# Edge sort of a graph network: bias by ScalarE, groups of four, and columns written a step later

## The reference

```
gate = sigmoid(silu(rbf @ W1 + b1) @ W2 + b2)     # rbf: edge_attr_64, 50000 x 64
msg  = gate * h[src]
aggr = segment_sum(msg, dst)
```

## Time and profile before

| what | value |
|---|---|
| three timed runs | 4744.28, 4751.31, 4754.04 us; median 4751.31 |
| profiled execution | span 4744.9 us from first to last instruction; the page gives no other time of it |
| busy over the span | TensorE 3915.0 us (83%), VectorE 3382.7 (71%), GpSimd 3071.7 (65%), ScalarE 1791.0 (38%) |
| the second pass of the sort | first matmul of its first group at 174.66 us, last scatter issued at 777.05 us |

### The profile page before, as it was taken

How to read it: one execution, slowest core, us unless ns; L and a number is a source line. 1 busy time by engine, 2 the same in 40 slices (tenths; PEclk the granted TensorE clock), 3 DMA queues, 4 the chain that set the end, 5 groups by cost and what they waited for, 6 DMA issues and landing times. The chain is left out here.

```text
span 4744.9 us, 105920 instructions
## 1 busy us (share of the span) xinstructions
PE 3915.0 (83%) x22300; PEld 3233.3 (68%) x22301; DVE 3382.7 (71%) x9318; ACT 1791.0 (38%) x5399; POOL 3071.7 (65%) x3178
## 2 busy tenths in 40 slices
PE   6799997889987889878899566779978778578886
PEld 3477775778776778767777556668866666366664
DVE  7799997667757778677787667874257778756666
ACT  0355553221123333333333100004257667367774
POOL 0266665777756777567775777766777773067774
PEclk9799998999998999989999777888978898778787
DMA  1233334856626445264452687861465444144445
GB/s 47 92 131 131 130 132 130 212 126 158 152 63 202 135 145 154 71 185 146 145 149 78 208 257 214 245 191 54 145 182 120 105 106 125 32 99 109 109 109 100
DMA packets 643665, 643.00 MB, mean 136 GB/s; under 512 B 314342, under 2 KB 549540, under 8 KB 643396
## 3 DMA queue, kind: packets, MB, share of 16 engines
q0 software_dynamic: 145840, 374.54, 27.8%
q1 hardware_dynamic: 443348, 213.36, 17.0%
q10 hardware_dynamic: 54336, 53.65, 3.3%
HBM read 470.09 MB, written 170.26 MB: 135 GB/s over the span
## 5 line engine op out<-in xcount | busy, mean ns | idle before, releaser
L1059 POOL DMA_INDIRECT G<-h_dram,idx x1572 | 1525.8, 971 | 556.8 <-issue 361.6
L1283 PEld LDWEIGHTS ps_a<-hotm,msg 128*128 128x128 f32 x4716 | 686.5, 193 | 196.2 <-DVE arena L1395 67.5
L1283 PE MATMUL ps_a<-hotm,msg 128*128 128x128 f32 x4716 | 730.0, 282 | 88.5 <-DVE arena L1395 87.8
L1271 PE MATMUL ps_e<-nnw,attT 128*128 128x256 f32 x2358 | 738.4, 396 | 76.8 <-DVE prodm L1388 42.4
L1395 DVE TENSOR_TENSOR arena<-ps_a,arena 128x256 f32 x1404 | 586.9, 418 | 218.8 <-issue 94.1
L735 POOL DMA_INDIRECT rec_dram<-rec,pos x392 | 376.7, 961 | 398.6 <-ACT rec L606 307.7
L1059 POOL DMA_INDIRECT G<-feat_dram,idx x420 | 402.4, 958 | 325.5 <-POOLq L241 197.9
L1317 ACT ACTIVATE msg<-prodm 128x256 f32<-128x256 f32 x786 | 327.5, 417 | 677.8 <-DVE prodm L1388 586.1
L749 POOL DMA_INDIRECT rec_dram<-rows,place x392 | 379.8, 969 | 222.1 <-issue 117.4
L1897 POOL DMA_INDIRECT arena<-rel_dram,idx x393 | 385.0, 980 | 128.6 <-issue 86.2
L1271 PEld LDWEIGHTS ps_e<-nnw,attT 128*128 128x128 f32 x2358 | 370.3, 195 | 118.4 <-DVE prodm L1388 56.4
(11 more groups left out here) (365 smaller groups left out, 7691.6 us busy)
## 6 DMA issues: line engine op xcount, KB each, us to landing
gate<-rec_dram SPq DMA_DIRECT2D x126, 384.0 KB
G<-msg_dram SPq DMA_DIRECT2D x300, 128.0 KB, 2.2
msg_dram<-msg ACTq DMA_DIRECT2D x270, 128.0 KB
rel_dram<-stage SPq DMA_DIRECT2D x25, 1040.0 KB
G<-h_dram,idx POOLq DMA_INDIRECT x1572
aT<-edge_attr SPq DMA_DIRECT2D x98, 128.0 KB
msg_dram<-arena ACTq DMA_DIRECT2D x90, 128.0 KB
attT<-attT_dram SPq DMA_DIRECT2D x74, 144.0 KB
```

Of the source, the lines that this page charges most:

```text
L1059: pool.indirect_dma_start(G[:, n % width, :], None, table, bass.IndirectOffsetOnAxis(ap=idx[:, which, n:n + 1], axis=0)).then_inc(sem(f"sw ...
L1271: t.matmul(ps_e[s % BANKS][:], attT[:, s // HU, s % HU, :], nnw[:], start=True, stop=True).then_inc(sem("ew"), 1)
L1283: last = t.matmul(ps_a[s % BANKS][:, h, :], of[:, h * P:(h + 1) * P], hot[:, s, :], start=True, stop=True)
```

## The change

In the second pass of the sort:

- The unit of the gate is the whole group. Lags are 0 and 1, `walk` has width 2. `sig` and `silu` hold four columns and move into the arena.
- ScalarE copies b2, now loaded to all partitions, into each `ps_g` bank after the gate has been taken from it; L641 and the three bf16 parts of b2 go. One matmul per bank of zeros comes once, at the start.
- One-hots of both keys are one comparison against `keys4` (the destination key three times, the source key once) and are made one step ahead.
- Fields, places and the copy of the 32 attributes are written in the step after their group's first layer. The places by source are kept as sums in `pos_s` and turned to integers once at the end.
- SyncE's wait and the loads are the same, with units of groups.

```diff
+                keys4 = area(4 * (EC + SG)).rearrange("p (c f) -> p c f", f=4)
+                pos_s = area(EC)
-                        for q in range(3):
-                            sp.dma_start(b2[32 * q:32 * q + 1, :], ...)
+                        sp.dma_start(b2[:], L1_gnn_b2.rearrange("(a d) -> a d", a=1).to_broadcast([P, D])).then_inc(sem("w_in"), 16)
...
+                def first_layer(b, h):
+                    return ps_z[b][:].rearrange("p j (q h e) -> p j q h e", q=2, h=DH)[:, :, :, h, :]
+                def by_pairs(of, b, h):
+                    return of[:, b, h, :, :].rearrange("p (j q) e -> p j q e", j=2)
... SyncE
-                                wait_ahead(sp, (sem("z"), upto(g * 2 + 1 - PAIRS)), (sem("a32"), upto(g - 2)))
+                                wait_ahead(sp, (sem("z"), upto(g - 2)), (sem("a32"), upto(g - 2)))
... ScalarE
+                        for c0, c1 in walk(nc.scalar, NG // 2, 0, 1, width=2):
+                            if c0:
+                                act.wait_ge(sem("z"), upto(g))
+                                act.wait_ge(sem("silu"), upto(g - 2))
+                                for h in range(DH):
+                                    last = nc.scalar.activation(by_pairs(sig, b, h), first_layer(b, h), ACT.Sigmoid, bias=b1[:, h:h + 1])
+                            if c1:
+                                for q in range(2):
+                                    if q == 0:
+                                        ... wait for sw_rec of the four columns
+                                        act.wait_ge(sem(f"attr_in{b}"), i * 32 + 32)
+                                    act.wait_ge(sem("g"), g * 2 + q + 1 + CREDIT)
+                                    nc.scalar.activation(rec[:, b, 2 * q:2 * q + 2, 0:D], ps_g[q][:], ACT.Sigmoid).then_inc(sem("gate"), 1)
+                                    act.wait_ge(sem("gate"), g * 2 + q + 1 + CREDIT)
+                                    nc.scalar.copy(ps_g[q][:], bias2).then_inc(sem("seeded"), 1)
+                                    if q == 0:
+                                        nc.scalar.copy(rec[:, b, :, WA32:WA32 + A32], at32[:, b, :, :]).then_inc(sem("a32"), 1)
... TensorE
+                        for c0, c1 in walk(nc.tensor, NG // 2, 0, 1, width=2):
+                            if c0:
+                                pe.wait_ge(sem("hot"), g + 1)
+                                ... the three rank matmuls
+                                pe.wait_ge(sem(f"attr_in{b}"), i * 32 + 32)
+                                pe.wait_ge(sem("silu"), upto(g - 2))
+                                ... first layer of four columns
+                            if c1:
+                                pe.wait_ge(sem("silu"), upto(g))
+                                for q in range(2):
+                                    pe.wait_ge(sem("seeded"), g * 2 + q + 1)
+                                    ... second layer of two columns
+                            if c0:
+                                pe.wait_ge(sem("looked_up"), g + 1)
+                                ... the four counting matmuls
... VectorE
+                        for c0, c1 in walk(nc.vector, NG // 2, 0, 1, width=2):
+                            if c0:
+                                ... lookup of places of g, then silu of g
+                                dve.wait_ge(sem("counted"), g + 2)
+                                one_hot_keys(g + 1, 1 - b).then_inc(sem("hot"), 1)
+                                ... sums of g
+                            if c1:
+                                ... fields and places of g - 1, after sw_rec of the four columns
+                        dve.wait_ge(sem("placed"), NG)
+                        v.tensor_tensor(place2[:], pos_s, trash2, ALU.add)
```

More of the change, by code:

```diff
@@ L386, in _ @@
                         sp.wait_ge(sem("x_in"), 32)
[L387 removed]
+                        sp.wait_ge(sem("w_in"), 16 * 6)
                     @block.gpsimd
@@ L588, in _ @@
                         credit(act, "a32", "sig", "gate")
-                        for c0, c1, c2 in walk(nc.scalar, NG // 2, 0, 1, 2, width=PAIRS):
-                            if c1:
[L591 to L614, removed]
@@ L622, in _ @@
                         credit(pe, "z", "g")
+                        for q in range(2):
+                            last = t.matmul(ps_g[q][:].rearrange("p j d -> p (j d)"), zerob[:],
+                                            identb[:].unsqueeze(1).to_broadcast([P, SG, P]), start=True, stop=True)
+                        last.then_inc(sem("primed"), 1)
                         t.matmul(ps_r[:], lt[:], four(hist[:]), start=True, stop=False)
                         t.matmul(ps_r[:], ones[0:K, :], four(base[0:K, :]), start=False, stop=True)
-                        for c0, c1, c2 in walk(nc.tensor, NG // 2, 0, 1, 2, width=PAIRS):
-                            if c1:
[L627 to L632, removed]
-                                    for j in range(2):
[L634 to L647, removed]
-                            if c0:
[L649 to L658, removed]
-                                    pe.wait_ge(sem("looked_up"), i * 2 + b + 1)
-                                    for j in range(SG):
-                                        last = t.matmul(ps_r[:, 0:j + 1, :], identb[:], four(OK[:, b, j, :], j + 1),
-                                                        start=False, stop=True, skip_group_check=True)
-                                    last.then_inc(sem("counted"), 1)
@@ L684, in _ @@
-                            if c1:
-                                n, i, s = c1
-                                dve.wait_ge(sem("sig"), upto(n))
-                                dve.wait_ge(sem("g"), upto(n - 2))
-                                for h in range(DH):
-                                    last = v.scalar_tensor_tensor(silu[:, s % 2, h, :, :], ps_z[s % 2][:, :, h * P:(h + 1) * P],
-                                                                  b1[:, h:h + 1], sig[:, s % 2, h, :, :], ALU.add, ALU.mult)
-                                last.then_inc(sem("silu"), 1)
@@ new lines, in _ @@
+                                dve.wait_ge(sem("hot"), g + 1)
+                                dve.wait_ge(sem("before"), g + 1)
+                                left = ps_r[:, :, 0:KD]
+                                v.tensor_tensor(moved[:], left, thr[:, 0:1, :].to_broadcast([P, SG, KD]), ALU.is_ge).then_inc(sem("moved"), 1)
+                                v.tensor_tensor(prod[:, b, :, KD:K], ps_r[:, :, KD:K], OK[:, b, :, KD:K], ALU.mult)
+                                dve.wait_ge(sem("moved"), g * 3 + 1)
@@ new lines, in _ @@
+                                dve.wait_ge(sem("sig"), upto(g))
+                                dve.wait_ge(sem("g"), (g - 1) * 2 + CREDIT)
+                                for h in range(DH):
+                                    last = v.scalar_tensor_tensor(by_pairs(silu, b, h), first_layer(b, h), b1[:, h:h + 1],
+                                                                  by_pairs(sig, b, h), ALU.add, ALU.mult)
+                                last.then_inc(sem("silu"), 1)
+                                dve.wait_ge(sem("counted"), g + 2)
```

131 lines of the change are left out of this document (67 added, 64 removed).

## The result

The changed kernel takes 4912.48 us (median of 4 runs, 4909.29 to 4916.88), the kernel before 4750.11 (4 runs, 4744.28 to 4754.04): a ratio of 1.0342 [1.0328, 1.0357], 3.4% slower.

What follows compares the result with a forecast made beforehand. The prediction took a loop through the late edge-column copy and the next loads to bound each step: 96 x (7.7 - 6.08) + 4 = 159.5 us on the 4744.9 us span, plus 6.4, gives 4911 us; range 4845 to 5010.

Steps and rivals of the forecast that it cites:

- The loop: From first layer through second-layer half, gate, copies and loads to the next first layer: 7.55 us a step, against TensorE's 5.62.
- The landing: Edge-column load from issue to landing: 2.0 us taken, bounds 1.7 and 2.8, plus 0.15 for TensorE's start.
- Bias copy: ScalarE's copy of 512 bias columns into a PSUM bank: 0.60 us taken, bounds 0.29 and 0.60.
- The clock: TensorE's clock dropping after idle time: 0.15 us a step on average, bounds 0 and 3.0.
- falls in most steps: Rival: TensorE's clock drops in most steps, costing some 1.5 us more, period 9.1, 5043 us; chance 0.12.
- TensorE alone: TensorE's own work per group once the bias matmuls go: 6.08 - 0.46 = 5.62 us.
- removed matmul decides: Rival: loads return in time, so the step is TensorE's 5.62 us and the kernel takes 4711 us; chance 0.06.
- the deciding point: Whether SyncE's wait for group g-2's edge-column copy is met a step later; the prediction read that it is.
- VectorE and GpSimd: Their work per step: about 5.1 and 5.0 us, not the bound; rival as new bound near 6.1, chance 0.02.
- One-hots a step ahead: VectorE making one-hots a step early: worth nothing, because TensorE waits for them neither before nor after.
- Setup: Block that ends when the load of X lands: 0 taken for VectorE's lost bias split, bounds -0.5 to +0.5 us.
- Tail: From the last first layer to the last scatter's end, eight scatters back to back: 16.5 us, so +4.

Runs made afterwards that it cites:

- Kernel 1: Changed kernel with the attribute load waiting only for the first layer, the edge-column load only for the copy, separate semaphores, TensorE waiting for attributes alone: 4692.98 us, 0.9888.
- 9: Kernel 1, but TensorE again waits for both loads to land, so only the issue of the loads is split: 4850.29 us, 1.0219.
- kernel 10: Kernel 1, but SyncE again holds both loads behind both waits, so only TensorE's wait on landing is split: 4879.76 us, 1.0279.
- kernel 2: Changed kernel with the edge-column copy moved ahead of the first gate in ScalarE's step: 4736.58 us, 0.9977.
- 3: Changed kernel with the edge-column copy moved between the first gate and its bias copy on ScalarE: 4851.53 us, 1.0217.
- kernel 5: Changed kernel with six unread bf16 filler matmuls on TensorE, ahead of its wait for the loads: 4878.93 us, 1.0287.
- kernel 4: Kernel before the change with only the edge-column copy moved later, behind the gate of its group's first pair: 4751.01 us, 1.0001.
- kernel 8: Kernel 1 with the next group's one-hots made last in VectorE's step, behind the fields: 4782.99 us, 1.0084.
- Kernel 7: Kernel 1 with the bias made by TensorE matmuls again, b2 loaded as one bf16-rounded row, no ScalarE bias copies: 4735.10 us, 0.9972.

## Why the prediction was right, step by step

The mechanism held, and with it the time: 4911 forecast, 4912.48 measured. Kernel 1 shows it from outside: take the edge-column copy out of TensorE's way and all of the loss is gone. Kernels 9 and 10 show that both the shared issue and the shared semaphore carry it.

- *The loop.* Forecast 7.55, found 7.32 as the mean of the short steps; the terms here are those of the turn shown, 7.35. First layer in one block: 1.09, not 2 x 0.65; the 0.65 of the earlier trace rows held a change of work on either side. Half the second layer with hand-over: 2.03, not 1.92. Gate, bias copy, edge-column copy: 1.44, as added up. SyncE 0.26 for 0.22, first issue 0.52 for 0.52. Landing with TensorE's start: 2.01 for 2.15. Over all short steps SyncE has 0.24 and the landing 1.98. The 0.15 for TensorE's start stood in no row, and no run shows it apart from the landing.
- *The landing.* It was a choice between 1.7 and 2.8 us. The Trainium skill, DMA: Bandwidth & Descriptors, section "Anatomy of one DMA", puts a DMA's fixed cost near 2 us. It says so of DMAs that GpSimd issues; for these, issued by SyncE, the traces have about that size, but not one fixed value: from issue to the matmul 1.98 us on average for 64 KB in the changed kernel, 2.22 to 2.33 in 9, 2 and 3, where scatters run beside it. Of undisturbed loads those of 128 KB take 2.16 us (kernel 10) and those of 64 KB 1.97 to 2.10. The 2.0 taken was right for this kernel; the expectations of 2, 3, 9 and 10 carried it over to shorter loops, and there it was 0.2 to 0.4 too short.
- *Bias copy.* Bounds 0.29 and 0.60, taken 0.60, measured 0.59 (L613). The Trainium skill, ScalarE: Activation LUTs, section "What ACT_TABLE_LOAD costs", gives 186 ns + 0.833 ns per element for an ACTIVATE with immediate scale and bias. Taken over to a copy of 512 columns that is 0.61 us, an estimate: the trace agrees, and also for the 128 columns of L615, 0.29.
- *The clock.* The term that was mis-sized: 0.15 us a step forecast, 25 x (8.88 - 7.32)/96 = 0.41 found. The rival "falls in most steps" had the mechanism and the size of one step right (1.56 for 1.5) and its frequency wrong: a quarter of the steps. These 39 us are what kernel 5 gives back, 26 to 37 us by the count taken. That the two errors, -0.23 and +0.26, cancelled is luck: the period of 7.7 is right as a sum and neither part as sized.
- *TensorE alone.* 5.62 forecast, 5.43 in kernel 1: first layer 0.21 and counting matmuls 0.10 shorter, second layer 0.12 longer. The rival "removed matmul decides" would have given 4711; with the loop open it is 4693. It was rightly given a small chance. But the prediction calls it the deciding point that the copy of group g - 2 is met a step later, and that is not enough. In kernels 2 and 4 it is met a step later as well; kernel 2 is 44 us behind kernel 1, and kernel 4 loses nothing against the kernel before. What decides is the length of the loop against TensorE's 5.43 us.
- *VectorE and GpSimd.* Forecast 5.1 and 5.0 us, under the bound. In kernel 1 they are busy for 107.27/119 x 5.43 = 4.9 and 86.39/119 x 5.43 = 3.9 us by the union of spans, and TensorE stays full. The silus of a group gave 0.33 us, 1.41 for 2 x 0.87, where 0.26 was the estimate.
- *One-hots a step ahead, "worth nothing".* Right for this kernel, as its loads covered everything, but as a statement on the edit it was wrong: kernel 8 shows it worth 90 us once the loop is open. In the new order of TensorE the counting matmuls end right ahead of the rank matmuls, and nothing covers a late one-hot.
- *Setup.* Forecast 0 (-0.5 to +0.5), found +2.9 at the start of the pass, 1.95 of it already at the start of the histogram. I looked at VectorE's work in that block and not at SyncE's queue, where 128 KB of broadcast bias had moved ahead of X, in place of three single rows. The other 0.9 us are not traced. Kernel 7, which loads one row, starts its pass at 170.79, earlier than the kernel before (171.74).
- *Tail.* 16.5 us forecast from the last first layer to the end of the last scatter, 942.70 - 925.89 = 16.8 found.

## What to carry to other kernels

When an edit moves the release of a buffer, write down the loop that it closes: release, issue, landing, use, and all work queued between that use and the next release; then compare its length with the step of the bounding engine. Two loads with one wait and one semaphore are as late as the later of both, and it takes both the issue and the landing apart to undo it: here that turned 3.4% slower into 1.1% faster. An edit that is worth nothing under one bound has to be priced again under the next. And a landing measured in one loop is no constant: in the shorter loops here it ran beside the scatters and took 0.2 to 0.4 us longer.

## What was not expected of the hardware

Short idle times that come back in every step cost TensorE its clock in some of the steps. With 1.8 us of idle time on average in front of the first layer, in a step of 7.3 us and busy for the rest, 25 of 96 steps ran long at the lower granted clock (0.66 in the stretch shown). With less of it they became fewer: 15 of 96 at 1.64 us (kernel 10), 5 at 1.51 (9), 4 at 1.50 (3), 1 at 0.53 (5), none without any (1); in kernel 2, at 0.33, the clock fell once. In the first four of these kernels a long step cost some 1.5 us, because half of a second layer stood in the loop.

The landing of one and the same 64 KB load was not expected to move either: 1.98 us in the changed kernel, 2.22 to 2.33 in kernels 2, 3 and 9, where most of the loads have packets of scatters beside them.
